# Two recurrent layers with attention between them: history stored by batch, attention two batches a step, layer 2's opening prepared in a written-out turn, f left out of each layer's first step

## What is computed

```python
def layer(x, h0, Wx, Wh, b):                 # c0 = 0
    for t in range(128):
        a = x[:, t] @ Wx + b + h @ Wh        # 4 gates of 128
        i, f, o = sigmoid(a[:, 0:H]), sigmoid(a[:, H:2*H]), sigmoid(a[:, 2*H:3*H])
        g = tanh(a[:, 3*H:4*H])
        c = f * c + i * g
        h = o * tanh(c)
x = x + attn(layer(x, cond, Wx1, Wh1, b1))   # per batch: (theta phi^T / sqrt(128)) g
h = layer(x, cond, Wx2, Wh2, b2)
x = x + relu(h @ W1 + b1) @ W2 + b2
```

## Time and profile before

| | us |
|---|---|
| median of 3 runs | 440.43 (440.18, 440.43, 443.11) |
| the profiled execution | 441.66 |
| its span, first to last instruction | 439.6 |
| PE busy in the span | 423.1 (96%), 5028 passes and products |
| DVE busy | 308.0 (70%) |
| ACT busy | 216.4 (49%) |
| POOL busy | 7.6 (2%) |
| DMA | 8.15 MB, mean 19 GB/s |

### The profile page before, as it was taken

How to read it: one execution, slowest core, us unless ns; L and a number is a source line. 1 busy time by engine, 2 the same in 40 slices (tenths; PEclk the granted TensorE clock), 3 DMA queues, 4 the chain that set the end, 5 groups by cost and what they waited for, 6 DMA issues and landing times.

```text
span 439.6 us, 14398 instructions
## 1 busy us (share of the span) xinstructions
PE 423.1 (96%) x5028; PEld 316.0 (72%) x5119; DVE 308.0 (70%) x1700; ACT 216.4 (49%) x1101; POOL 7.6 (2%) x19
## 2 busy tenths in 40 slices
PE   8999999999999999999989999999999999999997
PEld 6777666777766677766789777777777777777775
DVE  5877676666666766667656777777777777777774
ACT  3666555555545555555454444444444444444443
POOL 6000000000000000000000000000000000000000
PEclk9999999999999999999999999999999999999999
DMA  5010011111011111000000000000000000000000
GB/s 177 9 19 14 8 19 18 18 18 17 3 16 18 18 18 18 13 5 12 13 14 1 7 20 20 18 18 18 8 10 18 18 18 18 17 1 18 18 18 13
DMA packets 11692, 8.15 MB, mean 19 GB/s; under 512 B 1097, under 2 KB 11129, under 8 KB 11674
## 3 DMA queue, kind: packets, MB, share of 16 engines
q1 hardware_dynamic: 10874, 6.17, 7.1%
q0 software_dynamic: 512, 1.22, 0.9%
q10 hardware_dynamic: 288, 0.52, 0.4%
HBM read 2.87 MB, written 1.05 MB: 9 GB/s over the span
## 4 chain that ended last, share of the span: by engine, by line
PE 88%; ACT 5%; DVE 3%; issue 2%; DMA 1%; SPq 0%; DVEq 0%
PE fobank L419 18%; PE fobank L413 9%; PE bankV L399 8%; PE gibank L413 7%; PE bankU L389 6%; PE bankV L389 4%; PE gibank L377 4%; ACT fgate L761 4%; PE bankY L597 4%; PE fobank L377 4%; PE gibank L383 3%; PE fobank L383 3%; PE bankU L590 3%; PE bankY L481 2%; PE bankV L486 2%
## 5 line engine op out<-in xcount | busy, mean ns | idle before, releaser
L761 ACT ACTIVATE fgate<-fobank 128x16 f32<-128x16 f32 x256 | 46.9, 183 | 166.1 <-PE fobank L419 162.0
L419 PEld LDWEIGHTS fobank<-ring,whf 128*128 128x128 f32 x508 | 75.7, 188 | 69.6 <-DVE ring L933 62.2
L419 PE MATMUL fobank<-ring,whf 128*128 128x16 f32 x508 | 98.9, 270 | 3.3
L922 DVE TENSOR_TENSOR scan<-fgate,cell 128x16 f32<-128x16 f32 x256 | 45.4, 178 | 78.0 <-ACT fgate L761 75.7
L925 DVE TENSOR_TENSOR_SCAN cell<-scan 128x48 f32<-128x48 f32 x256 | 68.3, 267 | 11.4 <-ACT scan L768 0.3
L413 PEld LDWEIGHTS gibank<-h_hi,wh_parts 128*128 128x128 f16 x1016 | 65.3, 117 | 0.0
L772 ACT ACTIVATE ogate<-fobank 128x16 f32<-128x16 f32 x256 | 46.9, 183 | 33.2 <-PE fobank L383 0.7
L413 PE MATMUL gibank<-h_hi,wh_parts 128*128 128x16 f16 x1016 | 62.1, 169 | 0.0
L413 PE MATMUL gibank<-h_lo,wh_parts 128*128 128x16 f16 x1016 | 62.0, 169 | 0.0
L399 PE MATMUL bankV<-warm_x,zeros 128*128 128x512 bf16 x164 | 61.7, 376 | 0.0
L413 PE MATMUL fobank<-h_hi,wh_parts 128*128 128x16 f16 x508 | 52.8, 176 | 7.6 <-ACT fgate L761 0.4
(11 more groups left out here) (167 smaller groups left out, 550.9 us busy)
## 6 DMA issues: line engine op xcount, KB each, us to landing
rows_t<-rows SPq DMA_DIRECT2D x16, 128.0 KB
x_rows<-in_x_dram SPq DMA_DIRECT2D x17, 64.0 KB
out_dram<-y_sb SPq DMA_DIRECT2D x16, 64.0 KB
xres<-x2T SPq DMA_DIRECT2D x15, 64.0 KB, 1.9
xin<-x2T SPq DMA_DIRECT2D x14, 64.0 KB, 1.8
w<-in_L_ffn_W_dram POOLq DMA_DIRECT2D x2, 256.0 KB, 4.0
wh<-in_L_cond_Wh_dram ACTq DMA_DIRECT2D x1, 256.0 KB, 2.8
wx<-in_L_cond_Wx_dram ACTq DMA_DIRECT2D x1, 256.0 KB, 3.6
```

What stands on the lines that cost most here:

```text
L419: nc.tensor.matmul(step_out(p, t, GF), whf[layer][:], ring[:, (s - 1) % STEPS, :], start=False, stop=True, skip_group_check=True).then_inc ...
L761: nc.scalar.activation(fgate[:], fobank[p][:, NB * t:NB * t + NB], ACT.Sigmoid, scale=1.0 / Z_UNIT).then_inc(f_done[layer], 1)
L922: nc.vector.tensor_tensor(out=fc_slots, in0=fgate[:], in1=c_psum, op=ALU.mult).then_inc(scan_inputs[layer], 1)
```

## The change

1. **History by batch.** `hist` keeps chunks 0 and 1. The copy of the later chunks writes `hist_late[P, 16, 112]`, so that a batch's 112 times are contiguous for PE; the copy's own output now has a stride of 112 elements from batch to batch.
2. **Attention two batches a step.** Steps 2 to 9 of layer 2's turn 0 each do one `outer_pair` (all in `bankU`), steps 4 to 11 each one `attend_pair` and one `late_x2` of two batches. The projections and biases for the next chunks stand between the g, i products and the o products (`between`) in steps 4 to 11. Fillers are added in steps 1 and 13 to 15.
3. **Last turn of layer 1 written out on PE** (ACT and DVE keep their loop). Its second half prepares layer 2's biases and the products with h0 in place of layer 1's next chunk.
4. **First steps without f.** In step 0 of each layer ACT takes no sigmoid of f and DVE writes a zero for f*c. PE leaves out the product of h0 with f's weights; in layer 1 it does o before f.
5. Smaller: `same_batch` comes from `bankY` later; the product of an empty history in step 2 is left out; the last chunk's rows are made in two halves.

```diff
-        hist = sb("hist", [P, NCH, P])
+        hist = sb("hist", [P, 2, P])
+        hist_late = sb("hist_late", [P, NB, T - STEPS])
...
-            def step(layer, s, count, filler=1, o_parts=None):
+            def step(layer, s, count, filler=1, o_parts=None, between=None):
...
                 passes(h_lo, [GG, GI]).then_inc(gi_ready[layer], 1)
+                if between:
+                    between()
                 add_zeros(filler)
...
-            with pe.Fori(1, ITER) as i:
+            with pe.Fori(1, ITER - 1) as i:
                 for s in range(STEPS):
                     step(0, s, i * STEPS + s)
                     beside1(i, s)
-
-            pe.wait_ge(set2_ready, SET2)
-            for g in GATES:
-                bias_gate(1, 0, g)
+            for s in range(STEPS):
+                if s == CH:
+                    pe.wait_ge(set2_ready, SET2)
+                step(0, s, (ITER - 1) * STEPS + s)
+                beside1(ITER - 1, s, last=s >= CH)
...
-            def attend_quad(q):
-
-                pe.wait_ge(p_kept, 2 * q + 2)
+            def attend_pair(q):
+
+                pe.wait_ge(p_kept, q + 1)
                 if q >= 2:
                     pe.wait_ge(x2_done, q - 1)
-                elif q == 1:
-                    pe.wait_ge(p_kept, NB // 2)
-                for k in range(4):
+                for k in range(2):
                     last = nc.tensor.matmul((bankV, bankY)[q % 2][:, LATE * k:LATE * k + LATE],
-                                            p_batch[:, 4 * q + k, :],
-                                            hist_b[:, 4 * q + k, :], start=True, stop=True)
+                                            p_batch[:, 2 * q + k, :],
+                                            hist_late[:, 2 * q + k, :], start=True, stop=True)
...
+                    if 4 <= s < CH:
+                        last = project_gate(1, 1, GATES[s - 4], x2T[:, 1, :])
...
+                    if CH <= s < CH + 4:
+                        bias_gate(1, 0, GATES[s - CH])
...
-                    step(1, s, s, filler=0)
+                    step(1, s, s, filler=int(s < 2 or s > 12), between=between_passes(s))
...
+                if s in (2, 3):
+                    keep_warm(bankY, 2)
...
+                if opening:
+                    act.sem_inc(f_done[layer], 1)
+                else:
...
+                    kept = ring[:, CH * p:CH * p + CH, :]
+                    if isinstance(i, int):
+                        out = hist[:, p, :].rearrange("p (t b) -> p t b", b=NB)
+                    else:
+                        out = hist_late[:, :, bass.ds(i * STEPS + (p * CH - STEPS), CH)].rearrange("p b t -> p t b")
+                    nc.vector.tensor_copy(out, kept).then_inc(hist_done, 1)
...
-                nc.vector.scalar_tensor_tensor(out=late(x2T)[:, 4 * q:4 * q + 4],
-                                               in0=late(xT)[:, 4 * q:4 * q + 4], scalar=1.0 / Z_UNIT,
+                nc.vector.scalar_tensor_tensor(out=late(x2T)[:, 2 * q:2 * q + 2],
+                                               in0=late(xT)[:, 2 * q:2 * q + 2], scalar=1.0 / Z_UNIT,
...
-                if s in (7, 8, 9, 10):
-                    late_x2(s - 7)
+                if 4 <= s < 4 + NB // 2:
+                    late_x2(s - 4)
```

214 lines of the change are left out of this document (110 added, 104 removed).

## The result

| | before | after |
|---|---|---|
| median, us | 442.43 (20 runs, 440.02 to 446.16) | 438.63 (20 runs, 436.36 to 442.86) |
| the profiled execution | 441.66, span 439.6 | 441.85, span 439.8 |

The ratio is 0.9923, with a 95% interval of 0.9894 to 0.9952: 0.8% less time, 3.4 us by the ratio and 3.8 by the medians. That is within one per cent, and 438.63 lies above the range of 433.3 to 437.0. The median of before was 440.43 in the three executions that the prediction started from and 442.43 in twenty; both kernels scatter by several us from execution to execution, and most of what follows is about why. In every table a median is over all executions of a kernel, and a ratio is an estimate of its own, against executions of before made beside it and without the few that lie over 1.5% above their kernel's fastest.

What follows compares the result with a forecast made beforehand. The prediction read the kernel as bound by a chain of 256 steps, steadily 1.62 us each. Its terms 0.45 + 0.23 + 1.21 + 3.9 - 0.1 = 5.7 took the median from 440.43 to 434.7, range 433.3 to 437.0.

Steps and rivals of the forecast that it cites:

- start: Opening of layer 1: L419 of step 1 earlier by 0.45 us, and 0.23 from step 2.
- between the layers: Last h of layer 1 to first of layer 2: scores start sooner, no wait for f's sigmoid; 1.21 us gained.
- turn 0: Layer 2's first 16 periods: 1.2 us too much where it was 5.07, so 3.9 gained.
- copy: History copy on DVE, now writing with a stride: 0.39 us, still fits its slot; priced at 0.1 lost in all.
- four pairs taken away ahead of o's sigmoid: Layer 1's opening: mask, f's bias, h0 with f's weights, f's projection removed or moved behind; 1.4 us earlier first h.
- the fourteen passes owed behind it: PE work between o's first sigmoid and L419 of step 1: 1.54 us, so L419 at 11.55 instead of 11.89.
- the idle time that I named only as a lower bound: Layer 1's opening: a new idle between PE and o's sigmoid would leave a gain of 0.1 us instead of 0.45.
- The product of the empty history: Step 2: a 256-column product worth four passes goes, ten pass-equivalents become six; 0.23 us gained.
- The rival that the passes stay at 0.20: Layer 2's turn 0: attention passes stay at 0.20 us, 2.9 more; part of the dense-steps rival, chance 0.15.
- a copy of 0.6: Rival: the strided history copy overruns its slot by 0.13 us in 14 chunks, 1.8 in all, 436.5; chance 0.06.
- the written-out turn's instruction transfers: Rival: PE fetches instructions for the written-out turn; one fetch exposed by about 1.5 us gives 436.2; chance 0.05.
- The clock rival: Turn 0 without the filler: clock falls to 1.2 GHz, periods about 3.2 us; four cancel the gain; chance 0.03.

Runs made afterwards that it cites:

- before_warm8: The kernel before the change with eight warm-up products on PE in place of six, nothing else: 440.25 us, ratio 0.997 to the kernel before.
- combo_less_fill: Changed kernel with dense last turn of layer 1, eight warm-up products and `xin` issued earlier: 435.32 us, ratio 0.985 to the kernel before.
- before_again: The kernel before the change, unedited, profiled once more: span 440.8 us in one execution.
- again: The changed kernel, unedited, run and profiled once more: 438.08 us, ratio 0.993 to the kernel before.
- old_start: Changed kernel with layer 1's opening as before the change (f first, its sigmoid and f*c in step 0): 438.00 us, ratio 0.991.
- strided: Changed kernel with the history laid out by chunk again, two batches a step kept: turn 0 29.35 us, span 438.0 in one execution.
- padded: `unpadded` plus 80 increments of an unused semaphore between the eight warm-up products on PE: 446.12 us, ratio 1.009 to the kernel before.
- unpadded: Changed kernel with dense last turn of layer 1 and eight warm-up products, `xin` as in the changed kernel: 438.22 us, ratio 0.989.
- The four small edits: On the changed kernel: dense last turn of layer 1, eight warm-up products, earlier `xin`, attention-weight products and mask ahead of the wait for o's first sigmoid: 434.65 us.
- combo: Changed kernel with the four small edits together: 434.65 us, ratio 0.984 to the kernel before.
- combo_b: The same kernel as `combo`, run once more: 434.66 us, ratio 0.983 to the kernel before.
- dip_filled: Changed kernel with layer 1's last turn kept dense: zero products in steps 122 and 123, one h0 product moved to step 125: 437.53 us, ratio 0.988.
- warm8: Changed kernel with eight instead of six warm-up products ahead of the first transposition: 436.95 us, ratio 0.987 to the kernel before.

## Why the prediction missed

The forecast was 434.7 and the measured median 438.63, 3.9 us more. Three things make that up.

**The level it started from: 2.0 us.** The prediction subtracted its sum from 440.43, the median of three executions. The median of twenty is 442.43. Nothing in the three, 440.18, 440.43 and 443.11, said which of them was the usual one. So the step "the median becomes 440.43 - 5.7" would have missed by 2.0 with every term right.

**The terms: 1.2 us.** The sum was 5.7: start 0.68 (0.45 and 0.23), between the layers 1.21, turn 0 3.9, copy -0.1. Two kernels let me measure each term without the losses, both with an early clock: `before_warm8`, and `combo_less_fill`, which has the changed kernel's openings. They differ by 4.54 in span (437.91 and 433.37).

**The losses: 0.7 us.** The medians of before and after differ by 3.8 and not by these 4.5. That is a net figure, since before has losses of its own.

**Start: predicted 0.68, measured -0.63** (ninth h 23.36 and 23.99). This is the term that failed. It priced the same passes at two levels of the clock: four pairs taken away ahead of o's sigmoid at 0.43 a pair ("up to 1.7, less a part that DVE's scales now set; I take 1.4"), and the fourteen passes owed behind it at 0.11 each (1.54). At the low level the fourteen would have been 3.0 (an estimate from 0.43 a pair). Measured at either level, next to nothing or a loss is left:

- With the clock up by 7 us, the old opening has its first h at 10.02 and L419 at 10.33. The four pairs were worth 0.14 at o's sigmoid (9.18 and 9.04): it stands in ACT's queue behind `wh_parts` (L722 and L741, at 8.28 and 8.33), which waits for DVE's scale. The work behind it cost 0.94 at step 1 (10.33 and 11.27).
- With a late rise (`before_again` 13.28, `again` 12.76) the first h is 2.35 earlier (12.56 and 10.21), but L416 of step 1 stands at 13.28 against L419 at 13.38, and the ninth h at 26.00 against 26.33.

Two of the forecast places came true all the same: the first h near 10.1 (9.91 to 10.44 in seven profiles of the new opening, 10.97 in that of after) and, in the four of them with a rise before 7.1 us, the f product of step 1 at 11.21 to 11.62 for 11.55. But they were set against 11.58 and 11.89, and those two numbers held 1.6 us of TensorE's low clock. In the profile of after that product stands at 14.16. And the idle time that I named only as a lower bound (PE waiting for o's sigmoid) was there where the clock was early, 0.64 to 0.89 us. In the medians the opening is worth nothing (`old_start` 438.00, `again` 438.08). The product of the empty history, 0.23, came as forecast: the period at step 2 is 1.62 instead of 1.85.

**Between the layers: predicted 1.21, measured 1.14.** 3.90 instead of the forecast 3.8. L478 started at +0.23 as forecast; eight passes and the attention product followed to 223.65, and the projections began at +2.37 instead of +2.22.

**Turn 0: predicted 3.9, measured 4.11.** 26.87 against the forecast 27.1; attention passes 0.11 apart, `late_x2` 0.55, L944 at +1.02 and the next f*c branch 0.70 rather than 0.74 from h, so 1.72 for the forecast 1.75. The rival that the passes stay at 0.20 is out: `strided` shows what it would have cost, 2.48 (forecast 2.9).

**History copy: predicted 0.1, measured 0.07** (L1 193.04 and 193.11), which is not told from nothing: two profiles of the unchanged kernel have 193.13 and 193.00. The two rows of the copy in after:

```profile
L990 DVE COPY hist_late<-ring x14: 274/278/280, 52.5 to 222.4; 128x128 f32 x14
L990 DVE COPY hist<-ring x2: 220/221/222, 26.6 to 39.5; 128x128 f32<-128x128 f32 x2
```

0.28 instead of the 0.39 that I took from L1014's rate, and it fits. The Trainium skill's rule on 16-byte lines (SBUF — State Buffer, section Door 1: The DMA port swizzle) holds for both: the trace shows 0.06 us more for 128 scattered writes in one instruction, and `strided` 0.08 us more a pass for scattered reads on PE.

Two sums of the rivals don't come out, without a bearing on the forecast. With 1.46 more a period at half clock, four periods cancel the gain, but eight would give 446.4 and sixteen 458, not 441 and 452. And a copy of 0.6 in a slot of 0.42 is over by 0.18 and not 0.13, 2.5 us in fourteen chunks.

Steady periods are 1.62, as forecast. What I had not priced at all is this:

- **`xin`.** I had the written-out turn's instruction transfers as a rival, with 0.05, but as a fetch that PE waits for. In the profiles it came as a block that another transfer waits for. Of the seven profiles with the changed code and `xin` issued as before (`padded` aside) six show it, 1.0 to 1.5 us each and in `unpadded` 4.0 (with the fall of the clock that followed); none of the three of before does, where the block nearest to h of step 144 began 5.3 to 5.4 us ahead of it and the next 5.3 to 5.8 behind it. The change leaves `xin`'s issue where it was (0.73 after that h in both); it moves the code under it.
- **The clock in the last turn.** The clock rival put a fall into turn 0, for the missing filler. Turn 0 held 1.00. The fall came where 16-column products took the place of 128-column ones, which my count of passes held for equal work. L1 is 1.0 to 1.15 longer where it came, and the mean clock that goes with it stands in a third of executions with this turn.
- **The clock at the start.** Its record begins between 4.5 and 17 us, and the ninth h moves with it: 23.93 at 4.45 to 27.80 at 16.92 in the new opening, 23.36 at 5.16 to 26.33 at 13.28 in the old. No profile has the old opening with a rise near 16.9, so that the new one costs more there isn't shown; near 13 it was 0.3 ahead.

What stays open: why the clock rises when it does. With six warm-up products and the new opening the record begins at 10.24 or later in four of five profiles, with eight between 4.47 and 7.04 in all six (`padded` aside, where the products stand apart), but the same opening with six shows 4.45 and 16.94, and the old one with eight shows 5.16 and 9.82. And some executions have a low mean clock of which no profile tells the place. In before they are not rare: 12 of 69 executions made beside the runs read 0.983 to 0.987, with spans of 442.4 to 443.9, against 2 of 112 of all kernels with changed code (0.985 and 0.988). So a part of what the change gains in the mean may lie there, in a stretch that no term of the sum names.

## What to carry to other kernels

- Before a stretch at the start is priced, find out at which clock the row was taken, and take a second profile; price the passes that go and those that come at the same clock. A gain made of passes at 1.2 GHz is gone when the clock is up.
- Take the level to start from out of many executions: the median of three was 2.0 us under that of twenty here, half of the miss.
- When code is added or unrolled, blocks of instructions land elsewhere in time. A transfer that just makes its deadline can meet one; issue it a step earlier, which here was worth 1.0 to 4.0 us in six of seven profiles.
- When narrow products take the place of wide ones, look at the granted clock of that stretch in several executions. Here a filler in the same steps went with no fall there in seven profiles, and without it three of seven had one.
- The four small edits took the median from 438.63 to 434.65, as much as the change itself, and the spread of the spans from 6.5 us to 2.6 (eleven executions of `combo` and `combo_b`).

## What the runs showed of the hardware

- One 16 KB packet of instructions took 0.9 to 1.9 us in these profiles, and a sixteenth of the packets of a transfer under way waited for it to end: `xin` landed after 3.3 to 3.9 us instead of 1.8 in the six profiles with the stall.
- A wait of 1.34 us on PE was followed by 6.83 us at 1.2 GHz in one execution (`unpadded`), and waits of 0.8 to 1.3 us at the same place in `after`, `old_start`, `dip_filled`, `warm8` and `strided` were not followed by any fall.
- A semaphore increment on PE's queue takes about 0.09 us (`padded`: PE idle for 0.89 to 0.96 us at ten of them).
